# Two of four query/key/value products move ahead on TensorE in a fused Mamba-2 and attention/expert layer

## What is computed

```
xn = layernorm(x)
s  = mamba2 block(xn) + MLP block        # scan over 4 chunks of 128 tokens
g  = silu(attention + mixture of 4 experts (xn))
out = x + s * g
```

## Time and profile before

| | us |
|---|---|
| median of 3 runs | 859.13 |
| lowest, highest | 858.85, 860.33 |
| the profiled execution | 856.96 |
| its span (first to last instruction) | 855.1 |
| TensorE busy in the span | 784.8 (92%) |
| VectorE busy | 617.1 (72%) |
| ScalarE busy | 498.4 (58%) |
| GpSimd busy | 321.3 (38%) |

### The profile page before, as it was taken

The page is one execution under the profiler, slowest core; times in us unless marked ns, Lnnn a source line. Parts: engine busy times, 40 slices in busy tenths (PEclk is TensorE's granted clock), DMA queues, the critical chain, the costliest instruction groups (busy, mean ns, idle before and its releaser), DMA issues. The chain is left out here.

```text
span 855.1 us, 18101 instructions
## 1 busy us (share of the span) xinstructions
PE 784.8 (92%) x5472; PEld 481.4 (56%) x5472; DVE 617.1 (72%) x1469; ACT 498.4 (58%) x928; POOL 321.3 (38%) x600
## 2 busy tenths in 40 slices
PE   2779999999999989999899999999899998999997
PEld 1554564755547555665647555475556656474645
DVE  2686569685887858787696857878587876978634
ACT  2425784476753776557844667537764577446652
POOL 5423624054521716037250545217260372505400
PEclk9998999999999999999999999999999999999999
DMA  4000000000000100000000000000000000000000
GB/s 167 1 3 20 14 1 2 9 16 26 0 2 14 30 0 0 8 13 25 0 0 8 14 25 0 1 6 28 11 0 8 13 26 0 0 8 14 25 2 13
DMA packets 15145, 11.73 MB, mean 14 GB/s; under 512 B 1040, under 2 KB 13968, under 8 KB 14992
## 3 DMA queue, kind: packets, MB, share of 16 engines
q1 hardware_dynamic: 15120, 11.43, 4.4%
HBM read 7.76 MB, written 2.10 MB: 12 GB/s over the span
## 5 line engine op out<-in xcount | busy, mean ns | idle before, releaser
L1102 ACT ACTIVATE sb_pr<-S 128x768 f32<-128x768 f32 (+1 forms) x192 | 161.2, 878 | 130.0 <-PE S L445 129.4
L1198 DVE TENSOR_REDUCE sb_mx<-S 128x2 f32<-128x256 f32 (+3 forms) x256 | 198.1, 818 | 33.2 <-PE S L445 32.0
L1722 POOL TENSOR_SCALAR_AFFINE_SELECT sb_pr<-sb_pr 128x256 f32<-128x256 f32 (+1 forms) x192 | 98.1, 517 | 298.2 <-ACT sb_pr L1102 297.7
L445 PE MATMUL R<-sb_pr,sb_va 128*32 128x512 f32 (+3 forms) x1024 | 89.7, 445 | 6.2 <-ACT sb_pr L1102 3.4
L445 PE MATMUL R<-sb_W,sb_pr 128*128 128x96 f32 (+1 forms) x512 | 69.5, 276 | 0.0
L445 PE MATMUL R<-sb_xfT,sb_W 128*128 128x512 f32 x144 | 69.2, 602 | 0.0
L445 PE MATMUL S<-sb_kT,sb_qT 32*128 32x256 f32 (+3 forms) x512 | 56.3, 384 | 13.2 <-DVE sb_mx L1198 9.3
L445 PEld LDWEIGHTS R<-sb_W,sb_pr 128*128 128x128 f32 x512 | 63.5, 192 | 3.8 <-issue 3.5
L445 PEld LDWEIGHTS S<-sb_kT,sb_qT 32*128 32x128 f32 x512 | 27.5, 183 | 65.9 <-DVE sb_mx L1198 58.0
L1432 DVE SCALAR_TENSOR_TENSOR sb_x<-R,sb_wts,sb_x 128x96 f32<-128x96 f32 x128 | 40.6, 317 | 22.8 <-PE R L445 19.4
L445 PE MATMUL S<-sb_qT,sb_kT 32*128 32x256 f32 (+3 forms) x512 | 56.3, 384 | 0.5 <-ACT sb_pr L1102 0.5
(11 more groups left out here) (217 smaller groups left out, 1719.0 us busy)
## 6 DMA issues: line engine op xcount, KB each, us to landing
sb_xin<-x SPq DMA_DIRECT2D x9, 256.0 KB, 2.8
sb_W<-weights SPq DMA_DIRECT2D x1, 2290.0 KB, 10.4
sb_qT<-sb_mT SPq DMA_DIRECT2D x128, 4.0 KB
sb_xres<-x SPq DMA_DIRECT2D x8, 256.0 KB, 2.8
out<-sb_xres SPq DMA_DIRECT2D x7, 256.0 KB, 2.3
sb_cT<-sb_xact SPq DMA_DIRECT2D x8, 128.0 KB, 2.3
sb_W<-weights SPq DMA_DIRECT2D x1, 514.0 KB, 5.1
sb_cst<-consts SPq DMA_DIRECT2D x1, 328.0 KB, 3.0
```

The costliest lines, as they stand in the source:

```text
L445: return pe.matmul(o, lhsT, rhs, start=start, stop=stop, skip_group_check=True)
L1102: act.activation(pr[:, e % 4, :, 0:n], S[pair_of_exp(e)][:, :, 0:n], ACT.Exp).then_inc(p_sb, 1)
L1198: o = dve.tensor_reduce(mx[:, n // P - 1, g, heads[0]:heads[1] + 1], found[:, :, at_col:at_col + n], AX.X, ALU.max, negate=True)
L1722: pool.affine_select(out=keep, in_=keep, compare_op=ALU.is_ge, fill=0.0, base=0, pattern=pattern, channel_multiplier=-1)\
```

## The change

`project_qkv(r, t)` is one of the four products. It is called for t = 0 at the end of stage A, between `weigh_values` and `turn_y`, with two waits (for `xbT` and for the last exponential); for t = 1 between the turns of line 706 (709 after the change) and the output projection; for t = 2 and 3 where all four stood. In the head before the loop, which has no stage A ahead, t = 0 is called just before it. Nothing changes on the other engines, and no operation's size.

```
--- before.py
+++ after.py
@@ -689,6 +689,9 @@
                     pe.wait_ge(xc_sb, at(xc_sb, r, n))
                 mm(bank(t)[:, 0:DI + NH], xaT[:, t * P:(t + 1) * P], w("zdt")).then_inc(z_ps, 1)
 
+            def project_qkv(r, t):
+                mm(bank(t)[:, 0:3 * D], xbT[:, t * P:(t + 1) * P], w("qkv")).then_inc(qkv_ps, 1)
+
             def dense(o, n):
 
                 for _ in range(n):
@@ -705,6 +708,9 @@
                     for t in range(T):
                         i = pe.transpose(R[3][:, t * P:(t + 1) * P], oT[:, 1, t * P:(t + 1) * P], ident)
                     i.then_inc(ot3_ps, 1)
+                if head:
+                    project_qkv(r, 1)
+                if tail:
 
                     pe.wait_ge(yT_sb, at(yT_sb, r, 0))
                     for t in range(T):
@@ -715,8 +721,8 @@
                 if head:
                     pe.wait_ge(xbT_sb, at(xbT_sb, r, 0))
                     pe.wait_ge(p_sb, at(p_sb, r, 0))
-                    for t in range(T):
-                        mm(bank(t)[:, 0:3 * D], xbT[:, t * P:(t + 1) * P], w("qkv")).then_inc(qkv_ps, 1)
+                    for t in range(2, T):
+                        project_qkv(r, t)
                 if tail:
                     pe.wait_ge(ao3_sb, at(ao3_sb, r, 2))
                     transposes(R[0], lambda t: ao[:, t, :]).then_inc(aoT_ps, 1)
@@ -890,6 +896,9 @@
                         new_state(r, 0)
                         weigh_values(r, 2)
                 weigh_values(r, G * UNITS - 2)
+                pe.wait_ge(xbT_sb, at(xbT_sb, r, 1))
+                pe.wait_ge(p_sb, at(p_sb, r, G * UNITS))
+                project_qkv(r, 0)
                 turn_y(r, T - 1)
 
 
@@ -903,6 +912,8 @@
             pe.wait_ge(xab_sb, at(xab_sb, -2, 1))
             transposes(R[1], lambda t: xa[:, t, :]).then_inc(xaT_ps, 1)
             pe.wait_ge(wh_loaded, 16)
+            pe.wait_ge(xbT_sb, at(xbT_sb, -1, 0))
+            project_qkv(-1, 0)
             stage_b(-1, False, True)
             stage_a(-1)
             pe.wait_ge(wt_loaded, 16)
```

## The result

| | before, us | changed, us |
|---|---|---|
| median (6 runs each) | 859.12 | 853.91 |
| lowest, highest | 857.32, 861.33 | 851.99, 854.35 |
| profiled execution, its span | 856.96, 855.1 | 854.01, 852.3 |

The ratio is 0.9934, with a 95% interval of 0.991 to 0.9959. So it became faster by 0.66% (0.41 to 0.9%). On the median shown beforehand, 859.13, the ratio gives 853.46 us, 5.7 us less. The forecast was 854.8 with a range from 853.5 (859.13 - 5.6 = 853.53) to 857.2, so this lies just under the range. The ratio isn't the quotient of the two medians in the table; that is 0.9939 and stands for 5.2 us. A second comparison, with 10 runs of the changed kernel, gave 853.66 and a ratio of 0.9941 (0.9918 to 0.9963), so 5.1 us.

A forecast was written before the change was run, and what follows sets the result against it. TensorE, 92% busy, sets the pace, but idles 0.65 us before `turn_y` on the hand-over chain. Seven hand-overs by 0.62 us give 4.3 us: 859.13 - 4.3 = 854.8 us, range 853.5 to 857.2.

The forecast's parts named there:

- What bounds the hand-over: Between samples, a chain from `yz` through projection, products, evacuation, square and reduction to `x1n`; TensorE idles 0.65 us before `turn_y`.
- Part 1: First product moves into TensorE's idle 0.65 us before `turn_y`; `turn_y` delayed by 0, at most 0.10 us.
- absorbed by the branch: TensorE's loop branch between `turn_y` and line 706 would absorb up to 0.15 us of a late array.
- Part 2: Second product goes ahead of the projection: no TensorE time added or taken; projection 0.645 us later, 0.69 us VectorE slack left.
- Part 3: ScalarE empties two products early, then waits for the third; `aoT` and the chain behind it start 0.62 us earlier.
- the sum: Seven hand-overs by 0.62 us, 4.3 us in all, taken off the median of 859.13 us.
- Part 4: First hand-over unchanged; in the last stage one product is computed but never read, costing 0 to 0.10 us.
- case D: TensorE's clock dip before the loop, missing or doubled, worth 3.5 us either way; chance 0.03 as gain above 5.2 us.
- A: At `turn_y`, 0.10 to 0.35 us lost each time to draining or added waits; time 855.5 to 857.2 us; chance 0.13.
- B: No difference: TensorE's gap is not real or something unseen holds `x1n` back; 858 to 860 us; chance 0.09.
- C: Slower: the first product's new wait for `xbT` holds up `turn_y`; 866.1 us if `xbT` comes 2 us later; chance 0.03.

The follow-up runs named there:

- the kernel with that move alone: Changed kernel edited so that only one product moves ahead of the output projection and none ahead of `turn_y`: 859.84 us, ratio 1.001 to the kernel before.
- p1_only: Changed kernel edited so that only the first product moves, ahead of `turn_y`, the other three standing behind the projection: 854.31 us, ratio 0.9955 to the kernel before.

## Why the prediction was right, and where it was not

*What bounds the hand-over* was right. TensorE's idle 0.65 us were real, a product fitted in, and what came of it went through ScalarE and VectorE to `x1n` and TensorE.

*Part 1* was right. The product begins 0.79 us behind the start of the values product, as forecast (306.04 against 305.25). `turn_y` starts 0.09 us behind `yz` where it was 0.06, so 0.03 later, and line 709 is where line 706 was (0.64 behind `yz`). The new waits hold nothing up. That a delay would be absorbed by the branch was right in kind; the size was 0.33, not 0.15. The 0.15 came from comparing the hand-overs with and without the jump back, and so missed the 0.19 that both have. The Trainium skill's 108 ns for a compare-and-branch ("Advanced Engine Details and Errata", Control Flow Timing) would have put it lower still; the rows of the kernel before, with a median of 208 ns, don't agree with it, and they decide.

*Part 2*, "no time is added or taken", was shown by the kernel with that move alone, and its slack (0.69 forecast, 0.67 measured) too.

*Part 3* was mis-sized by a little: I took 0.62 us, by adding ScalarE's steps, and it is 0.65, TensorE's figure. Counted from `yz`, the third tile's evacuation was forecast at 4.40 us and came at 4.38, and the two tiles then took 1.27 us in place of 1.28. Seven times 0.03 is 0.2 us of the sum.

*Part 4* held. The product that nobody reads costs nothing to see: `turn_y` in the last hand-over is at 0.09 behind `yz`, and `x1n` at 6.23, as before.

*The step that failed* is the treatment of the clock. It stands in two places. In the sum, the 2.17 us between the profiled execution and the median were carried over unchanged, as if both kernels had the same. And case D named only the dip at 67 to 74 us, read the loop as free of dips from a mean over 744 us, and said that it "should be the same in both kernels".

What the runs showed in its place: that distance of 2.17 us is at least in part the slow stretches. They differ from run to run, 0 to 3 in the loop at 1.3 to 1.4 us each, and the part ahead of the loop ended anywhere from 105.16 to 109.33 us in the five traces of the two kernels. A median of few runs holds some of them. The mechanism gave what was forecast: the rows give 4.55 us for the change where the sum had 4.3, a ratio of 0.9947, which lies in both intervals. The measured ratios of 0.9934 and 0.9941 mean 5.7 and 5.1 us. So of the 1.4 us between 5.7 and the forecast's 4.3, 0.2 are Part 3 and some 1.1 are not the hand-over's.

The record has a mean granted clock for 79 runs of the kernel before and for 16 of the changed one in the two comparisons. Time falls by about 0.55 us with each 0.001 of clock. The means lie 5.2 us apart, and at equal clock, by a straight line through both, 4.6 us (95%: 4.2 to 5.0). That speaks for the clock as what lies above the rows' figure. It doesn't show it: the same line puts `p1_only` 3.8 us under the kernel before, though its rows have the same 0.65 us, so this way of reading is good to about 1 us. Whether the changed kernel has fewer slow stretches or had luck in these runs stays open; in the traces it has 5 in 21 samples, and the one before 3 in 14. The range's lower end took only 0.4 us for all this, too little on a kernel whose runs spread by 4 us; with the same room below as above, the end would have been 852.4.

*The rivals.* A (part is lost) fell with the hand-over's 0.65 us. B fell with the same row. C did not occur, with `xbT` ready at 304.48 and the product at 305.09. D did occur, as stretches past 104 us, in both kernels. In the changed kernel's first trace they took back more than half of the gain. D had also stood, with a chance of 0.03, for a gain of more than 5.2 us: by the ratio of 0.9934 the gain is above that, by the second comparison it is not. The Trainium skill says ("TensorE: Matmul & The Clock Gate", The HAM clock gate) that where the clock changes varies from run to run. The changed kernel's slow stretches lay in the first and sixth, again the first and sixth, and then the second sample, and the kernel before had none and then three: this agrees, though the place within the sample did not vary.

## What to carry to other kernels

An idle gap ahead of a wait is worth filling with work that is already due later on the same engine; its worth is the length of that work, as far as the gap holds it, times the number of gaps, if what follows on that engine is on the path. Here the order of the rest brought nothing by itself. After such a move look for the new idle time it makes on the next engine: here ScalarE's 1.06 us, and half a square put into it brought another 2.9 us. Where a loop's clock can fall at a weak place, compare rows counted from a common event, count the slow stretches by the distance from sample to sample and not by a mean over the whole loop, and give the range as much room as the runs spread.

## What I had not expected of the hardware

- The granted clock fell to 0.50 in the middle of the loop although TensorE was busy 2.29 to 2.62 of the 3 us before and no wait there was longer than 0.34 us. Each time cost 1.3 to 1.4 us.
- Between the turns on the two sides of the loop's branch TensorE lost 0.33 us where the array had run dry (0.19 where the loop was left), and nothing where 0.43 us more of work stood ahead.
- The same square in two halves costs ScalarE 0.63 + 0.64 us in place of 1.07, so 0.2 us more in busy time, and is faster all the same since the first half is free.
